# The end of an attention stage: who normalises the router's rows, how many row scatters follow each tile, and where the weight splits stand

## The reference

```python
x = x + _L0_xattn_ref(ctx_1024, _layernorm(x), ...)   # memory shift and a strided convolution
x = x + _L0_ffn_ref(_layernorm(x), ...)               # shared expert + 2 of 8 routed experts
x = x + _L1_xattn_ref(_layernorm(x), ctx_1024, ...)   # 16 heads over 64 context rows
x = x + _L1_ffn_ref(_layernorm(x), ...)               # 2 of 8 experts, gated

def _L1_ffn_ref(x, Wr, W1, W2, W3):
    gate_logits = xf @ Wr
    w, idx = jax.lax.top_k(gate_logits, 2)
    w = jax.nn.softmax(w, axis=-1)
    ...
    y = jnp.einsum('neh,ehc->nec', jax.nn.silu(h) * g, W2)
    out = jnp.einsum('nec,ne->nc', y, comb)
```

## Time and profile before

| | us |
|---|---|
| runs (3) | 947.77, 940.98, 950.99 |
| median | 947.77 |
| the profiled execution, its own time | 939.47 |
| its span, first to last instruction | 937.7 |
| granted TensorE clock, mean over the span | 0.938 |

### The profile page before, as it was taken

How to read it: one execution, slowest core, us unless ns; L and a number is a source line. 1 busy time by engine, 2 the same in 40 slices (tenths; PEclk the granted TensorE clock), 3 DMA queues, 4 the chain that set the end, 5 groups by cost and what they waited for, 6 DMA issues and landing times.

```text
span 937.7 us, 16483 instructions
## 1 busy us (share of the span) xinstructions
PE 797.2 (85%) x4534; PEld 679.2 (72%) x4534; DVE 542.9 (58%) x1418; ACT 457.8 (49%) x1301; POOL 429.6 (46%) x398
## 2 busy tenths in 40 slices
PE   2989975999996899899998976487989999999991
PEld 1636634886884788888997865476978988888891
DVE  5847736643554788897887975346323333355352
ACT  1458643664664777777775664132323333333330
POOL 2201555635861788777442487613673222222221
PEclk9799996999997999999998986599999999999996
DMA  8899974876996833632703312232342222255524
GB/s 258 277 311 314 319 248 147 270 230 149 234 237 225 199 58 62 177 76 54 200 2 101 126 69 91 86 113 74 120 137 81 69 63 67 90 180 181 168 91 151
DMA packets 122019, 143.09 MB, mean 153 GB/s; under 512 B 10295, under 2 KB 113516, under 8 KB 120908
## 3 DMA queue, kind: packets, MB, share of 16 engines
q1 hardware_dynamic: 92056, 93.61, 33.4%
q0 software_dynamic: 19856, 38.95, 15.3%
q10 hardware_dynamic: 10022, 9.48, 3.1%
HBM read 71.28 MB, written 70.71 MB: 151 GB/s over the span
## 4 chain that ended last, share of the span: by engine, by line
PE 52%; POOL 15%; issue 9%; DVE 9%; DMA 5%; ACT 5%; DVEq 2%; SPq 1%; ACTq 0%; POOLq 0%
PE psum L662 25%; PE psum L1012 13%; POOL xs_dram L587 7%; PE psum L951 3%; PE psum L931 3%; POOL pr L581 3%; ACT pr L1282 2%; POOL N L602 2%; PE psum L1022 2%; PE psum L841 2%; DMA fx<-xs_dram 2%; POOL X L539 1%; PE psum L999 1%; DMA X<-in_x_dram 1%; DVE sm L1938 1%
## 5 line engine op out<-in xcount | busy, mean ns | idle before, releaser
L607 POOL DMA_INDIRECT yk_dram<-ys,L x71 | 67.9, 956 | 204.6 <-ACT ys L1357 200.9
L2050 DVE TENSOR_TENSOR hs<-psum,hs 128x384 f32<-128x384 f32 x71 | 39.6, 558 | 168.0 <-PE psum L1012 141.1
L539 POOL DMA_INDIRECT X<-yl_dram,slots_y x64 | 101.2, 1581 | 35.7 <-issue 15.0
L1012 PE MATMUL psum<-whi,xTh 128*128 x284 | 103.7, 365 | 12.2 <-DVE xTl L2068 12.2
L1282 ACT ACTIVATE pr<-psum,nmx 128x64 f32<-128x64 f32 x512 | 108.0, 363 | 11.5 <-DVE nmx L1933 11.0
L514 POOL DMA_INDIRECT xs_dram<-N,slots x64 | 64.8, 1013 | 98.8 <-DVEq L1628 59.0
L662 PE MATMUL psum<-w_sb,cz 128*128 x426 | 104.3, 381 | 5.1 <-ACT ys L1357 5.1
L581 POOL TENSOR_TENSOR pr<-pr,sm 128x1024 f32<-128x1024 f32 x32 | 62.7, 1961 | 82.7 <-DVE sm L1940 80.0
L1012 PE MATMUL psum<-whi,xTl 128*128 x284 | 96.6, 340 | 0.0
L1012 PE MATMUL psum<-wlo,xTh 128*128 x284 | 96.5, 340 | 0.0
L662 PEld LDWEIGHTS psum<-w_sb,cz 128*128 128x128 f32 x426 | 75.4, 190 | 13.8 <-issue 6.4
(11 more groups left out here) (328 smaller groups left out, 1923.1 us busy)
## 6 DMA issues: line engine op xcount, KB each, us to landing
fx<-xs_dram SPq DMA_DIRECT2D x80, 130.0 KB, 3.8
xs_dram<-fill SPq DMA_DIRECT2D x4, 2600.0 KB, 17.3
yl_dram<-fy SPq DMA_DIRECT2D x80, 128.0 KB
xs<-xs_dram SPq DMA_DIRECT2D x71, 130.0 KB, 2.1
wlo<-in_L_ffn_W_dram SPq DMA_DIRECT2D x4, 1536.0 KB, 13.4
ym<-yk_dram ACTq DMA_DIRECT2D x12, 512.0 KB, 5.3
xs_dram<-cz SPq DMA_DIRECT2D x1, 5200.0 KB, 26.6
xs_dram<-cz SPq DMA_DIRECT2D x8, 650.0 KB, 6.6
```

Of the source, the lines that this page charges most:

```text
L539: po.indirect_dma_start(X[:, t, :], None, YL[b // 2], bass.IndirectOffsetOnAxis(ap=slot_y[k][:, t:t + 1], axis=0), compute_op=ALU.add).the ...
L607: po.indirect_dma_start(YK, bass.IndirectOffsetOnAxis(ap=yid[:, j:j + 1], axis=0), ys[j % YB], None).then_inc(s[f"y_out{j % YB}"], 16)
L1012: last = nc.tensor.matmul(bank[2 + 2 * half + b][:, 0:H1], a[b][:, c, :], w, start=c == i == 0, stop=c == DC - 1 and i == 2)
L2050: tt(hs[j % 2], bank[4 + j % 2][:, 0:H1], hs[j % 2], ALU.mult).then_inc(s["e_hg"], 1)
```

## The change

It has five parts.

1. **Rows.** `rows_in` of router tiles 16 to 31 goes from GpSimd to ScalarE, with a semaphore of its own (`n_ra`): tiles 16 and 17 behind `expo` of round 31, 18 and 19 in round 32, 20 to 23 in round 33, and 24 to 31 between `high(2)` and `high(3)` behind the loop.
2. **Scatters.** The router's steps of the first half come a round earlier (`RANKED` 25, router tiles 12 to 15 turned in rounds 21 and 22, `choice` in rounds 21, 22 and 24, the last batch's statistics in 17 to 20), and its scatters go out four per tile in rounds 27 to 30. Behind the loop stand `second(0)` and then all 16 scatters of the second kind.
3. **Splits and collects.** `split_high` and `split_low` of the next batch's pieces come a round earlier; `collect` goes two per tile from round 2 on, and so ends in round 14 and not 16.
4. **Weight parts.** `high(0)` and `high(1)` go to rounds 32 and 33, `low(0)` to round 33, and `low(1)` behind the loop, after the copy of the router's logits.
5. **Second half.** The end of `rest_places`, with `positions(1)`, becomes `rest_final` in tile 6 of VectorE; GpSimd scatters the second half from tile 5 on, and `second(1)` is in tile 9.

```diff
-    17: (7, 8), 18: (9,), 19: (10,), 20: (11,), 22: (12, 13), 23: (14, 15), 32: (16, 17), 33: (18, 19)}
+    17: (7, 8), 18: (9,), 19: (10,), 20: (11,), 21: (12, 13), 22: (14, 15), 32: (16, 17), 33: (18, 19)}
-RANKED = 26
+RANKED = 25
+AFTER = {31: (16, 17), 32: (18, 19), 33: (20, 21, 22, 23)}
...
                 for m in TURNS.get(n + 1, ()):
-                    rows_in(m)
-                if n >= 2 and (n - 2) // BT < NB - 1:
-                    b, r = (n - 2) // BT, (n - 2) % BT
+                    if m < GM:
+                        rows_in(m)
+                if n >= 1 and (n - 1) // BT < NB - 1:
+                    b, r = (n - 1) // BT, (n - 1) % BT
...
-                for _ in range(3 if n < 2 else 2 if n < 8 or n % 2 or n == 16 else 1):
+                for _ in range(3 if n < 2 else 2):
...
-                if n == 28:
+                if n == RANKED + 2:
                     po.wait_ge(s["rout"], LG + 1)
                     po.wait_ge(s["xs_fill"], 16 * YB)
-                    scatter(0, 0, 5)
-                if n == 29:
-                    scatter(0, 5, 10)
-                if n == 30:
-                    scatter(0, 10, GM)
+                if RANKED + 2 <= n < RANKED + 6:
+                    scatter(0, 4 * (n - RANKED - 2), 4 * (n - RANKED - 2) + 4)
             second(0)
-            scatter(1, 0, 4)
-            for m in TURNS[TILES + 1]:
-                rows_in(m)
-            for m in range(LEFT, LEFT + QT):
-                rows_in(m)
-            scatter(1, 4, 8)
-            for m in range(LEFT + QT, TILES):
-                rows_in(m)
-            scatter(1, 8, GM)
+            scatter(1, 0, GM)
...
-                if j == 4:
+                if j == 5:
                     po.wait_ge(s["rout"], LG + 2)
...
+            def rows_in(m):
+                if m % BT == 0:
+                    ac.wait_ge(s["n_q"], CHAINS[m // QT])
+                act(N[:, m, 0:D], X[:, m, :], ACT.Identity, scale=rstd[:, m:m + 1], bias=nshift[:, m:m + 1]).then_inc(s["n_ra"], 1)
...
-                    if n == TILES - 1:
+                    if n == TILES:
                         high(0)
-                    if n == TILES:
+                    if n == TILES + 1:
                         high(1)
+                    for m in AFTER.get(n, ()):
+                        rows_in(m)
...
                 high(2)
+                for m in range(LEFT + QT, TILES):
+                    rows_in(m)
                 high(3)
...
-                    if n == 18:
+                    if n == 17:
                         routed_norm(3, 0)
                         routed_norm(3, 1)
...
-                    if n == TILES:
+                    if n == TILES + 1:
                         low(0, 1)
-                    if n == TILES + 1:
-                        low(1, 2)
...
+                low(1, 2)
                 low(2, 3)
                 low(3, 4)
...
                         rest_places()
+                    if j == 6:
+                        rest_final()
```

More of the change, by code:

```diff
@@ L266, in build @@
             l_ga l_gb
-            n_st n_q n_r t_p xt_a ro_p ro_sb
+            n_st n_q n_r n_ra t_p xt_a ro_p ro_sb
             spa spd r_m r_pt rout sc1 sc2
@@ L625, in _ @@
                         collect(b_, k_, t_, t_ + 1)
-                if n == 28:
+                if n == RANKED + 2:
                     po.wait_ge(s["rout"], LG + 1)
                     po.wait_ge(s["xs_fill"], 16 * YB)
-                    scatter(0, 0, 5)
-                if n == 29:
-                    scatter(0, 5, 10)
-                if n == 30:
-                    scatter(0, 10, GM)
-            second(0)
-            scatter(1, 0, 4)
-            for m in TURNS[TILES + 1]:
-                rows_in(m)
-            for m in range(LEFT, LEFT + QT):
-                rows_in(m)
-            scatter(1, 4, 8)
-            for m in range(LEFT + QT, TILES):
-                rows_in(m)
-            scatter(1, 8, GM)
+                if RANKED + 2 <= n < RANKED + 6:
+                    scatter(0, 4 * (n - RANKED - 2), 4 * (n - RANKED - 2) + 4)
+            second(0)
+            scatter(1, 0, GM)
             for j in range(SA):
                 spread(j)
-                if j == 4:
+                if j == 5:
                     po.wait_ge(s["rout"], LG + 2)
-                if 4 <= j < 8:
-                    scatter(0, GM + 4 * (j - 4), GM + 4 * (j - 4) + 4)
-                if j == 8:
+                if 5 <= j < 9:
+                    scatter(0, GM + 4 * (j - 5), GM + 4 * (j - 5) + 4)
+                if j == 9:
                     second(1)
-                if 8 <= j < 12:
-                    scatter(1, GM + 4 * (j - 8), GM + 4 * (j - 8) + 4)
+                if 9 <= j < 13:
+                    scatter(1, GM + 4 * (j - 9), GM + 4 * (j - 9) + 4)
         @block.tensor
@@ L983, in attention @@
                 for m in range(LEFT, TILES):
-                    pe.wait_ge(s["n_r"], m + 1)
+                    pe.wait_ge(s["n_ra"], m - GM + 1)
                     turn_rows(m, m % QT)
@@ L1903, in rest_places, with rest_final @@
                 ve.drain()
+            def rest_final():
+                cm = cmp[:, 0:nrest * E].rearrange("p (j e) -> p j e", e=E)
                 tt(te[:, :], te[:, :], e_f[:, :], ALU.subtract)
@@ L1986, in between @@
                         chain(n - 14, ((8, 12),))
-                    if n == 18:
+                    if n == 17:
                         routed_norm(3, 0)
                         routed_norm(3, 1)
-                    if 19 <= n < 22:
-                        chain(n - 19, ((12, 16), (24, 32)), 3)
+                    if 18 <= n < 21:
+                        chain(n - 18, ((12, 16), (24, 32)), 3)
+                    if n == 21:
+                        choice(0, 0, 0, 11)
                     if n == 22:
-                        choice(0, 0, 0, 8)
-                    if n == 23:
-                        choice(0, 1, 0, 8)
+                        choice(0, 1, 0, 11)
                     if n == RANKED - 1:
-                        choice(0, 0, 8, GM)
-                        choice(0, 1, 8, GM)
+                        choice(0, 0, 11, GM)
+                        choice(0, 1, 11, GM)
                         counted(0)
@@ L2006, in between @@
                         full_places()
-                    if 29 <= n < 32:
-                        chain(n - 29, ((16, 24),))
+                    if 28 <= n < 31:
+                        chain(n - 28, ((16, 24),))
                 xlow(0)
```

6 lines of the change are left out of this document (3 added, 3 removed).

## The result

The changed kernel takes 917.39 us (median of 4 runs, 914.57 to 918.69), the kernel before 944.38 in the runs beside it (4, 940.27 to 950.99). The ratio is 0.9704, with a 95% interval of 0.9634 to 0.9774. Later, on another chip, 916.36 (6 runs) stood against 941.81 (11 runs): 0.9728 (0.9692 to 0.9765), 25.4 us. The profiled executions are 918.69 and 939.47, 20.8 apart. The first pair of medians lies 27 apart because the median of before lay above its profiled run; the argument goes by the profiled ones.

The account below looks back on a forecast made before the run. GpSimd's work up to the last row scatter was taken to bound the gap between attention and experts. Rounds 8.4, gap 12.0 and experts 2.3 sum to 22.7 us, from 947.77 to 925.1 (profiled execution 916.8); range 915 to 938.

Parts of the forecast that it names:

- the 4.27 of that stall: Third wait of `values` for GpSimd's split: 4.27 us, about 2 of it put down to VectorE's late operand, 2.2 counted as gain.
- they fit, nothing is charged: Two collects in each of rounds 8 to 14 were to leave GpSimd 0.45 us of some 7.7, at no cost.
- The lower bound of 5: Least gain from earlier splits in the attention's rounds: only the waits, the third worth nothing, with the give-back; 5 us.
- The gap: Between attention and first turned expert tile: scatters come last at 594.6 instead of 606.63, a gain of 12.0 us.
- the pair in the middle: Two neighbouring `low` of VectorE, near 574 and 577, meeting the second-half scatters: taken to block them for 6 us together.
- The rule weighed: Scatters' descriptors wait while VectorE's `low` holds the shared port; if spared, scatters would end near 580 and the router would bound.
- the loss by the buffers: In the experts, `ys` held by later `spread`, counted to `ys(19)`: a loss of 2.2 us against a gain of 4.5.
- A: Rival: in the gap, weight parts hold the scatters or rows slow ScalarE's copies; 17 us gained, 931; chance 0.17.
- B: Rival: in the attention's rounds, VectorE or GpSimd replaces the split's stalls; 8.4 becomes 1, 15 us gained, 933; chance 0.10.
- C: Rival: scatters not blocked, the router bounds the gap, all clock comes back; near 30 us gained, 918; chance 0.08.
- D: Rival: experts start and stay at TensorE's low clock, 3 us more a tile; twelve tiles give 961; chance 0.03.
- E: Rival: scatters slip behind `scale(31)`, rows delay `phigh`, both attention ends stay; 8 us gained, 940; chance 0.07.

## Why the prediction was right

The profiled execution was forecast at 916.8 and took 918.69, the median at 925.1 and 917.39. The mechanism was right in all three stages. That the total came so near is in part luck: the three stages gained 23.6 us for 22.7, because part 3 lost 1.25 in round 1 that was not charged while the gap gained 1.5 more than forecast, and the untouched code ahead of them took 2.8 back. The sizes, step by step:

*Part 3.* 8.4 forecast, 7.7 between the traces, 7.5 undone alone. No `values` waits for the split any more. By tiles, a step being the time from the start of one tile's `values` to that of the next: the step at tile 8 went from 9.87 to 7.41 us (2.5 gained, 2.3 forecast); at tiles 16 and 17 3.8 (2.8 net of the statistics); at tiles 23 to 25 2.9 (3.3). Of the 4.27 of that stall 2.00 now stand at `values(23)` for VectorE's operand and 1.38 at `values(24)`, where the prediction left 2, but the step at tile 24 is at full clock again. The term that was missed is in round 1: "they fit, nothing is charged" was worked out for rounds 8 to 14 alone, but round 1 now holds three collects and a split, `scale(2)` came 3.09 behind its sums instead of 1.83, and the step at tile 2 went from 8.25 to 9.50. That is 1.25 lost. The lower bound of 5 doesn't follow from what stands beside it either: 2.3 and 2.3 less 0.8 are 3.8.

*Part 2.* `scale(31)` was forecast within 0.3 us of the sums being ready, and it starts 0.4 behind their end (546.35 and 1.22; 547.98), 0.1 behind the reciprocal. No scatter of the loop is over 1.3.

*The gap.* 12.0 forecast, 13.5 between the traces. First second-half scatter 8.39 behind the sums of tile 31 (8.0 forecast); drain 4.70 for 4.4; blocked beyond 0.97: 2.92, 2.96, 2.00 and 1.99, together 9.87 for 11.4; last scatter 37.3 behind the sums (38.6), first expert tile 4.52 behind its start (4.72). `route` ends 38.9 behind the sums (40.9), 3.0 ahead of the tile (some 2). The largest error is the blocking: the pair in the middle became three parts back to back, since the first of them began 2.3 us later than forecast, behind the copy of the router's logits, and ScalarE was through with the last high part 1.8 earlier; and when a scatter is let go between two parts the next is blocked for the second part only from its own start on. From the end of `values(31)` to the first expert tile it is 26.4 us, not 28.4.

*Which part of it did what.* The rows on ScalarE are worth 11.3 us, four scatters a tile 2.7; the new place of the first two weight parts minus 1.7, by one pair of traces on the uneven chip. Together that is 12.3 of the gap's 13.5. The router's steps a round earlier were not undone by themselves, and what they are worth stays open. The prediction didn't price the place of the weight parts by itself. It put the start of `values(30)` 2.9 behind the sums of tile 31, which it is, 4.5 before; none of that was on the path to the first expert tile, which goes through the scatters.

*The rule weighed.* It was predicted that the subtraction of a weight part, an operation with two inputs in SBUF, blocks the scatters. It does, 3.89, 3.93, 2.97 and 2.96 us for 0.96, and cutting it removes the stretch. The Trainium skill's page "SBUF — State Buffer", section "A bandwidth-pool intuition that's wrong (but worth ruling out)", describes such blocking for a copy on VectorE, up to about 115 ns behind its end. For a subtraction the trace agrees that there is blocking to the end of VectorE's instruction, but the scatter's own ends 0.84 us behind it. The section "🔬 SBUF: two separate sides", with its limit to GpSimd work that reads SBUF, did not spare the scatters; whether they count as such work, since they take their rows and places from there, these runs don't decide.

*Part 5.* 2.3 forecast, 2.4 between the traces, 2.8 undone alone. TensorE stands 1.58 behind tile 5 (1.5 forecast), and `ys` is held until tile 17 as forecast. Counted from `ys(0)`, `ys(5)` is 4.5 us earlier than before and `ys(19)` 2.1, so the loss by the buffers was 2.4 (2.2). The clock can move the stage by 1.4 alone, as the run with part 5 undone showed.

*The rivals.* A (17 gained) is out: VectorE's parts keep their 3.35, 9.88 for three, and ScalarE's copies theirs. B is out: beyond the 2.00 at `values(23)` for VectorE's operand, which the forecast had left standing, nothing took the splits' place but the 1.25 of round 1. C was not reached, since the scatters were blocked; its router bound is real. D did not come, the experts ran at 0.95 and 0.97 in the two long windows, and at 1.00 from 706 to 900 (the last 16 us of the second window have no work of TensorE):

```profile
588.00:686.00 98.00, 85.28 (x454) 74.81 (x455) 42.17 (x146) 29.82 (x83) 44.21 (x47) 0.95 0.36 114
706.00:916.00 210.00, 191.11 (x1074) 170.69 (x1072) 86.71 (x200) 67.16 (x185) 46.99 (x49) 0.97 0.38 118
```

E is out by the place of `scale(31)`.

*The median.* It was taken as 8.3 above the profiled execution, as for the runs of before that were shown; the changed kernel's is 1.3 below. The seven and eleven later runs of before have medians of 940.27 and 941.81, close to the profiled 939.47: the three runs shown lay high, and the forecast carried that over.

## What to carry to other kernels

When a serial engine sets a gap, count its own arithmetic first: moving rows to an engine with air in the same stretch brought four times what regrouping the transfers did. Price the second bound before you free the first: scatters that ended 7.0 and 9.2 us earlier were worth 3.4 and some 3.3 here, because the router stood 3 us behind, and where it stands moves by up to 3 us with the clock of a few products ahead of it. A step moved "into free rounds" must be checked in the first and the last round of its range, and so must the borders of lists that share a round.

## What the runs showed of the hardware

A drain on GpSimd with indirect transfers behind it costs 4.70 us until the next one starts, in every kernel here that has it behind the attention (4.1 to 4.2 in the experts), though the copy ahead of it waits until the earlier scatters have landed; a wait for the copy's own semaphore costs 0.28. An indirect scatter issues every 1.27 us, also beside ScalarE's high parts, but one that begins under VectorE's subtraction ends 0.84 us behind that. The point at which TensorE's clock falls differs from one execution of the same program to another: the router ended 38.9, 38.6 and 35.9 us behind the sums of tile 31 in three traces of the changed kernel. The same program took 7% longer on one of the chips, in waits for which the trace has no releaser, while the changed kernel's rounds and gap differed by under 1%. Two of the three variants tried there, though, had such a wait in the very gap, and needed another chip.
